# Second attention: when TensorE takes up the values of a quad, one quad behind each place or two behind every second

## The chip, the cores and the metric

The kernel runs on one core of a Trainium2 chip. The metric is the device time of one execution in microseconds (us); for the kernel before it is the median of three runs. One further execution was profiled.

## The reference, cut to what matters

Two layers, each with an attention and a feed-forward part. The change lies in the second layer's attention: two batches of 1,024 tokens, 32 heads of 16, one key and one value head shared by all, causal.

```python
def _L1_attn_ref(x, wq, wk, wv, wo):
    B, T, C = x.shape                      # 2, 1024, 512
    q = (x @ wq).reshape(B, T, 32, 16)
    k = x @ wk                             # one key head of 16
    v = x @ wv
    scores = jnp.einsum('bqhd,bkd->bhqk', q, k) * scale
    scores = jnp.where(causal[None, None], scores, -jnp.inf)
    probs = jax.nn.softmax(scores.astype(jnp.float32), axis=-1)
    out = jnp.einsum('bhqk,bkd->bqhd', probs, v).reshape(B, T, C)
    return out @ wo
```

## The kernel before, in words

The program has four stages, one behind the other: an opening with the first attention (to about 1160 us), a middle part, the second attention (`attention1`, from 1463 us, with its exponentials from 1500 to 2021 us), and a closing part.

`attention1` works in 16 **steps** (`STEPS1`), each four heads of one batch. A step has 12 **quads** (`QUADS`), one for each pair of half of the queries (`qc`, 512 columns) and key tile of 128 rows (`kt`) that the causal mask leaves: quads 0 to 3 have `qc` 0, quads 4 to 11 have `qc` 1. On the diagonal the width falls: quads 0 to 3 are 512, 384, 256 and 128 query columns wide, quads 4 to 8 are 512 wide, and quads 9, 10 and 11 are 384, 256 and 128.

Four kinds of work meet on a quad:

- **Maxima** (`maximum`, L1769 and L1774): scores with the queries as rows, written to one of two double banks `as_mxp`, from which VectorE takes a row maximum (L1707 where the whole width is below the diagonal, L1709 elsewhere). They are made 32 tiles ahead, for the next step, two in each place.
- **Scores** (`score`, L1752, with L1754 and L1755 for the mask): keys as rows, one of three banks `as_scp`. A quad has four of them, one for each head (two in quads 2, 3, 10 and 11, which take two heads in one bank). ScalarE takes the exponential of each into a ring `as_prob` of 24 (L1659).
- **Values** (`values`, L1793): per quad, four matmuls of 32 columns of the array side by side, one for each head, from `as_prob` into `as_op`. The type is float32, and the trace shows eight matmuls for a quad.
- **The copy out** (`copy_out`, L1666): `as_op` is a single bank. When the values of quad 3 and of quad 11 are in, ScalarE copies it to `as_u_sb`. The values of quads 0 and 4 (`kt == 0`) overwrite the bank, so they wait for that copy: `pe.wait_ge(s["u_copied"], 2 * t + qc)`.

The order on each engine is written out by hand. TensorE goes through 192 **places** (`QSETS`, index `g`; `n` is `g` modulo 12). A place is: a maximum, two scores, a maximum, two scores (maxima of the coming step, scores of quad `n`), and behind them values of earlier quads, by the lines that the change touches. ScalarE has its own list:

```python
for n in range(QUADS):
    if n == TURN_AT and t + 1 < STEPS1:
        maxima_out(t + 1)
    exps(t, n)
    if n == 2 and t >= 1:
        copy_out(t - 1, 1)
    if n == 6:
        copy_out(t, 0)
```

So the copy for quads 4 to 11 of the step before stands behind the exponentials of quad 2, and the copy for quads 0 to 3 behind the exponentials of quad 6. Score `x` waits until the exponential of score `x - 3` is done, maximum `u` until VectorE is done with maximum `u - 2`.

Of the kernel before, what the change touches and what calls it, by code (L numbers as in the profile page):

```python
# [600 lines left out]
QUADS = UNITS // G  # L601
# [972 lines left out]
def attention1(nc, k, q_dram, sums, recips, stale, queries_in, next_loads):  # L1574

    with ExitStack() as ctx:
# [22 lines left out]
        with nc.Block() as block:  # L1599
# [130 lines left out]
            def _(pe):  # L1730
                def score(t, n, j):
                    qc, kt = QK[n]
                    x = t * SCORES1 + FIRST1[n] + j
                    c0 = max(kt - 4 * qc, 0) * P
                    w = HALF - c0
                    jj, both = j % 2, UNITS1_OF[n] == 2
                    rows, group = slice(RG * jj, RG * jj + MAXROW + 1), slice(RG * jj, RG * (jj + 1))
                    if both:
                        out = scp[x % BANKS1][:, 0:PAIRS * w].rearrange("p (i c) -> p i c", i=PAIRS)
                        queries = q[t % SLOTS1][rows, :, HALF * qc + c0:HALF * (qc + 1)]  # L1740
                        block = out[:, :, 0:P]
                        after = lambda part: k.tri[group, 2 + part, :].unsqueeze(1).to_broadcast([RG, PAIRS, P])
                    else:
                        s0 = min(c0, HALF - 2 * P)
                        out = scp[x % BANKS1][:, s0:HALF]
                        queries = q[t % SLOTS1][rows, j // 2, HALF * qc + s0:HALF * (qc + 1)]
                        block = scp[x % BANKS1][:, c0:c0 + P]
                        after = lambda part: k.tri[group, 2 + part, :]
                    diagonal = kt >= 4 * qc
                    if x >= BANKS1:  # L1750
                        pe.wait_ge(s["exp_done"], x + 1 - BANKS1)
                    mm = nc.tensor.matmul(out, k.keys[rows, t // NG, kt * P:(kt + 1) * P], queries, start=True, stop=not diagonal)  # L1752
                    if diagonal:
                        nc.tensor.matmul(block, k.tri[group, 0, :], after(0), start=False, stop=False)  # L1754
                        mm = nc.tensor.matmul(block, k.tri[group, 1, :], after(1), start=False, stop=True)  # L1755
                    mm.then_inc(s["sc_ready"], 1)

                def maximum(u):
                    t, (i, qt, part) = u // MSTEP, MPAIRS[u % MSTEP]
                    full = qt >= 4 and part == 0  # L1760
                    k0 = HALF if qt >= 4 and part == 1 else 0
                    w = HALF if full else (qt % 4 + 1) * P
                    if u % MSTEP == 0:
                        pe.wait_ge(q_in[t % SLOTS1], MOVES * (t // SLOTS1 + 1))
                    freed(pe, ("max", u))
                    tile = mxp[banks["max", u][0]]
                    for jj in range(2):
                        rows = slice(RG * jj, RG * jj + MAXROW)
                        mm = nc.tensor.matmul(tile[:, jj, 0:max(w, 2 * P)], q[t % SLOTS1][rows, i, qt * P:(qt + 1) * P],  # L1769
                                              k.keys[rows, t // NG, k0:k0 + max(w, 2 * P)], start=True, stop=full)  # L1770
                    for half in () if full else range(2):
                        for jj in range(2):
                            group = slice(RG * jj, RG * (jj + 1))
                            mm = nc.tensor.matmul(tile[:, jj, w - P:w], k.tri[group, half, :], k.tri[group, 4 + half, :],  # L1774
                                                  start=False, stop=(half == 1))
                    mm.then_inc(s["mx_ready"], 1)

                def turn_maxima(t):
                    pe.wait_ge(s["mx_joined"], t + 1)
                    freed(pe, ("turn", t))  # L1780
                    nc.tensor.transpose(mxp[banks["turn", t][0]][0:G * TILES, 0, 0:P], mxd[:, t % 2].rearrange("p j i q -> p (j i q)"),
                                        k.ident[:]).then_inc(s["mt_ready"], 1)

                def values(t, n):
                    qc, kt = QK[n]
                    c0 = max(kt - 4 * qc, 0) * P
                    x = t * SCORES1 + FIRST1[n]
                    pe.wait_ge(s["exp_done"], x + UNITS1_OF[n])
                    if kt == 0 and 2 * t + qc > 0:
                        pe.wait_ge(s["u_copied"], 2 * t + qc)  # L1790
                    for j in range(G):
                        p0 = c0 if UNITS1_OF[n] == G else j // 2 * (HALF - c0)
                        mm = nc.tensor.matmul(op[2 * HD * j:2 * HD * (j + 1), c0:HALF], k.vn[:, t // NG, kt, :],  # L1793
                                              prob[:, (x + j % UNITS1_OF[n]) % RING1, p0:p0 + HALF - c0],
                                              start=(kt == 0), stop=(kt == 4 * qc + 3))
                    mm.then_inc(s["pv_done"], 1)
# [3 lines left out]
                for g in range(QSETS):  # L1800
                    t, n = divmod(g, QUADS)
                    if n == TURN_AT and t + 1 < STEPS1:
                        turn_maxima(t + 1)
                    if n == 0:
                        pe.wait_ge(m_in[t % SLOTS1], 32 * (t // SLOTS1 + 1))
                    mine = range(LEAD + MQUAD * g, min(LEAD + MQUAD * (g + 1), MSTEP * STEPS1))
                    for i in range(MQUAD):
                        for u in mine[i:i + 1]:
                            maximum(u)
                        for j in range(2 * i, min(2 * i + 2, UNITS1_OF[n])):  # L1810
                            score(t, n, j)
                    if g % 2 and g >= 3:
                        values(*divmod(g - 3, QUADS))
                        values(*divmod(g - 2, QUADS))
                for g in (QSETS - 2, QSETS - 1):
                    values(*divmod(g, QUADS))
# [303 lines left out]
```

## Time and profile before

| | |
|---|---|
| median of three runs | 2172.82 us (2171.63 to 2172.96) |
| the profiled execution, its own time | 2168.36 us |
| its span, first to last instruction | 2166.6 us |
| TensorE busy | 1990.0 us, 92% of the span |
| VectorE, ScalarE, GpSimd busy | 1161.2, 885.1 and 480.5 us |
| mean granted TensorE clock | 0.944 of full speed |

The span has 34,181 instructions. The profile calls TensorE's matmuls PE and its weight loads PEld, VectorE DVE, ScalarE ACT, GpSimd POOL. "Busy" of PE is the union of matmuls whose ends are modelled, so its idle time is better read as the distance between the starts of its instructions. In a timeline row the first number is the start, the second the length of the merged group, xN the number of instructions in it, and a bracket at the end tells the idle time ahead of it and what ended that.

### The profile page before, as it was taken

What the parts mean: (1) busy time and instruction counts of PE and PEld (TensorE: products, weight loads), DVE (VectorE), ACT (ScalarE), POOL (GpSimd) and SP (SyncE); (2) the same over time, 40 slices, a digit from 0 to 9 for tenths busy, and PEclk for the clock granted to TensorE, in tenths of its full rate; (3) what the DMA queues carried; (4) which work ended last, traced back from release to release, by engine and by line L of the source; (5) the groups of instructions that cost most, each with busy time, mean ns of one, the idle gap of its engine ahead of it and who ended that gap; (6) DMA issues with size and microseconds to landing.
All of it is one profiled execution on the core that took longest, in us unless ns stands there. A gap on an engine that the chain in (4) does not pass through costs nothing. (4 is left out here: it accounts for less than half of the span.)

```text
span 2166.6 us, 34181 instructions
## 1 busy us (share of the span) xinstructions
PE 1990.0 (92%) x12648; PEld 1151.5 (53%) x12648; DVE 1161.2 (54%) x2541; ACT 885.1 (41%) x1877; POOL 480.5 (22%) x376
## 2 busy tenths in 40 slices
PE   5859999999999999999967999988999999999698
PEld 4535666666666666666634454544444444444244
DVE  3536655555555555555402445437667667663166
ACT  3413344444444444444431222222666666666222
POOL 0014245555444444455330000000000000000000
PEclk8869999999999999999988999995999999998799
DMA  9742233222233323332135211153223212211201
GB/s 311 263 143 59 60 79 80 66 59 56 68 80 80 79 70 80 79 80 62 39 119 179 73 63 48 60 132 93 42 33 52 47 33 52 47 18 27 89 29 49
DMA packets 113592, 172.19 MB, mean 79 GB/s; under 512 B 26186, under 2 KB 46826, under 8 KB 113298
## 3 DMA queue, kind: packets, MB, share of 16 engines
q1 hardware_dynamic: 112402, 169.75, 29.7%
q8 instruction: 100, 1.64, 0.3%
q14 instruction: 66, 0.54, 0.1%
q10 hardware_dynamic: 1024, 0.26, 0.1%
HBM read 84.32 MB, written 29.38 MB: 52 GB/s over the span
## 5 line engine op out<-in xcount | busy, mean ns | idle before, releaser
L886 ACT ACTIVATE at_prob<-at_scp 128x512 f32<-128x512 f32 (+1 forms) x608 | 349.8, 576 | 515.5 <-PE at_scp L989 514.3
L1659 ACT ACTIVATE as_prob<-as_scp 128x512 f32<-128x512 f32 (+2 forms) x640 | 309.0, 563 | 200.2 <-PE as_scp L1755 148.9
L921 DVE CUSTOM_DVE_ANT_0 at_junk<-at_mxp,causal 128x128 f32<-128x128 f32 (+3 forms) x512 | 243.6, 488 | 189.9 <-PE at_mxp L1000 185.2
L1709 DVE TENSOR_REDUCE as_mxd<-as_mxp 128x2 f32<-128x256 f32 (+3 forms) x256 | 203.5, 821 | 98.3 <-PE as_mxp L1774 96.0
L916 DVE TENSOR_REDUCE at_mxf<-at_mxp 128x1 f32<-128x512 f32 x256 | 176.1, 688 | 142.7 <-PE at_mxp L1000 138.9
L1694 POOL TENSOR_TENSOR l_att_t<-l_att_t,as_spread 64x1024 f32<-64x1024 f32 x16 | 37.9, 2367 | 861.5 <-DMA as_spread<-l_recips 861.5
L1707 DVE TENSOR_REDUCE as_mxf<-as_mxp 128x2 f32<-128x1024 f32 x128 | 151.0, 1221 | 60.3 <-PE as_mxp L1769 60.1
L816 POOL TENSOR_TENSOR at_pre<-at_prob 128x512 f32<-128x512 f32 x64 | 80.2, 1282 | 409.8 <-ACT at_prob L886 409.8
L816 POOL TENSOR_TENSOR at_pre<-at_pre,at_prob 128x512 f32<-128x512 f32 x128 | 160.6, 1285 | 3.6 <-ACT at_prob L886 1.2
L1793 PE MATMUL as_op<-as_prob,l_vn 128*32 128x512 f32 (+3 forms) x1536 | 160.4, 540 | 0.0
L985 PE MATMUL at_scp<-hd_early_q,l_khi 97*128 97x512 f32 (+1 forms) x304 | 138.1, 454 | 10.9 <-DMA hd_late_q<-at_slo 8.2
L1022 PE MATMUL at_op<-at_prob,l_cn 128*32 128x512 f32 (+3 forms) x1536 | 143.7, 491 | 4.0 <-ACT at_u_sb L857 4.0
L985 PE MATMUL at_scp<-at_qhi,l_khi 97*128 97x512 f32 (+1 forms) x304 | 138.7, 456 | 0.8 <-ACT at_prob L886 0.5
L1000 PE MATMUL at_mxp<-l_khi,hd_early_q 96*128 96x512 f32 (+2 forms) x384 | 125.6, 381 | 10.2 <-DMA hd_early_q<-at_shi 8.9
L1000 PE MATMUL at_mxp<-l_khi,at_qhi 96*128 96x512 f32 (+2 forms) x384 | 122.5, 367 | 0.5 <-DVE at_mxf L916 0.2
L988 PE MATMUL at_scp<-hd_late_q,l_khi 96*128 96x512 f32 (+1 forms) x304 | 118.4, 389 | 0.0
L989 PE MATMUL at_scp<-hd_early_q,l_klo 96*128 96x512 f32 (+1 forms) x304 | 118.0, 388 | 0.0
L988 PE MATMUL at_scp<-at_qlo,l_khi 96*128 96x512 f32 (+1 forms) x304 | 116.8, 384 | 0.0
L989 PE MATMUL at_scp<-at_qhi,l_klo 96*128 96x512 f32 (+1 forms) x304 | 116.3, 383 | 0.0
L1769 PE MATMUL as_mxp<-l_keys,hd_early_q 48*128 48x512 f32 (+2 forms) x384 | 97.7, 488 | 19.2 <-DVE as_mxf L1707 7.3
L1752 PE MATMUL as_scp<-as_q,l_keys 49*128 49x512 f32 (+2 forms) x320 | 108.1, 463 | 7.8 <-ACT as_prob L1659 6.4
L1752 PE MATMUL as_scp<-hd_early_q,l_keys 49*128 49x512 f32 (+2 forms) x320 | 103.7, 446 | 5.7 <-ACT as_prob L1659 4.3
(232 smaller groups left out, 3352.8 us busy)
## 6 DMA issues: line engine op xcount, KB each, us to landing
hd_late_q<-at_slo SPq DMA_DIRECT2D x96, 128.0 KB, 2.4
at_qhi<-at_shi SPq DMA_DIRECT2D x96, 128.0 KB, 2.4
at_qlo<-at_slo SPq DMA_DIRECT2D x96, 128.0 KB, 2.4
hd_early_q<-at_shi SPq DMA_DIRECT2D x84, 128.0 KB, 2.5
at_spread<-l_recips SPq DMA_DIRECT2D x64, 128.0 KB, 2.8
l_o<-at_u_sb SPq DMA_DIRECT2D x16, 512.0 KB, 3.3
hd_early<-in_wmod SPq DMA_DIRECT2D x7, 1024.0 KB, 7.8
hd_late<-l_o SPq DMA_DIRECT2D x12, 512.0 KB, 4.4
```

The source lines that it names most:

```text
L816: nc.gpsimd.tensor_tensor(pre[:, j, :], other, prob[:, (x + j) % RING0, :], ALU.add).then_inc(s["pre_done"], 1)
L886: nc.scalar.activation(prob[:, x % RING0, c0:HALF], scp[x % BANKS0][:, c0:HALF], ACT.Exp).then_inc(s["exp_done"], 1)
L916: nc.vector.reduce_max(mxf[:, j, qt - 4:qt - 3], tile[:], AX_X).then_inc(s["mx_done"], 1)
L921: nc.vector.tensor_tensor_reduce(out=junk[:, u % 2, 0:w], in0=tile[:, 0:w], in1=k.causal[:, HALF - w:HALF], scale=1.0, scalar=LOWEST, op0= ...
L985: nc.tensor.matmul(out, k.khi[0:KR + 1, b, ks], q_cols(qhi[t % 2][0:KR + 1]), start=True, stop=False)
L988: nc.tensor.matmul(out, k.khi[0:KR, b, ks], q_cols(qlo[t % 2][0:KR]), start=False, stop=False)
L989: nc.tensor.matmul(out, k.klo[0:KR, b, ks], q_cols(qhi[t % 2][0:KR]), start=False, stop=True).then_inc(s["sc_ready"], 1)
L1000: nc.tensor.matmul(bank("max", t, u)[:, 0:w], qhi[t % 2][0:KR, qt // 4, j, qt % 4 * P:(qt % 4 + 1) * P], k.khi[0:KR, t // NG, k0:k0 + w], ...
L1659: nc.scalar.activation(prob[:, x % RING1, cols], scp[x % BANKS1][:, cols], ACT.Exp).then_inc(s["exp_done"], 1)
L1709: nc.vector.reduce_max(mxd[:, t % 2, :, i, qt:qt + 1], tile[:, :, 0:(qt % 4 + 1) * P], AX_X).then_inc(s["mx_done"], 1)
L1752: mm = nc.tensor.matmul(out, k.keys[rows, t // NG, kt * P:(kt + 1) * P], queries, start=True, stop=not diagonal)
L1793: mm = nc.tensor.matmul(op[2 * HD * j:2 * HD * (j + 1), c0:HALF], k.vn[:, t // NG, kt, :], prob[:, (x + j % UNITS1_OF[n]) % RING1, p0:p0 + ...
```

## The change

Before, a place with odd `g` ended with the values of the two quads `g - 3` and `g - 2`, and one with even `g` had no values. After, every place from `g` = 2 on ends with the values of quad `g - 2`. Nothing else is changed; ScalarE, VectorE, GpSimd and the DMA queues issue what they did, in the order they did.

```diff
                         for j in range(2 * i, min(2 * i + 2, UNITS1_OF[n])):
                             score(t, n, j)
-                    if g % 2 and g >= 3:
-                        values(*divmod(g - 3, QUADS))
+                    if g >= 2:
                         values(*divmod(g - 2, QUADS))
                 for g in (QSETS - 2, QSETS - 1):
                     values(*divmod(g, QUADS))
```

TensorE's order in places 6 and 7 of a step, before. L1769 and L1774 are maxima, L1752 scores, L1793 the values, here of quads 4 and 5 together:

```order
L1769 MATMUL as_mxp<-l_keys,hd_early_q 128x512 x2
L1752 MATMUL as_scp<-hd_early_q,l_keys 128x512 x2
L1769 MATMUL as_mxp<-l_keys,hd_early_q 128x512 x2
L1752 MATMUL as_scp<-hd_early_q,l_keys 128x512 x2
L1769 MATMUL as_mxp<-l_keys,hd_early_q 128x512 x2
L1774 MATMUL as_mxp<-l_tri 128x128 x4
L1752 MATMUL as_scp<-hd_early_q,l_keys 128x512 x2
L1769 MATMUL as_mxp<-l_keys,hd_early_q 128x512 x2
L1774 MATMUL as_mxp<-l_tri 128x128 x4
L1752 MATMUL as_scp<-hd_early_q,l_keys 128x512 x2
L1793 MATMUL as_op<-as_prob,l_vn 32x512 x8
```

And the same two places as they are now:

```order
L1769 MATMUL as_mxp<-l_keys,hd_early_q 128x512 x2
L1752 MATMUL as_scp<-hd_early_q,l_keys 128x512 x2
L1769 MATMUL as_mxp<-l_keys,hd_early_q 128x512 x2
L1752 MATMUL as_scp<-hd_early_q,l_keys 128x512 x2
L1793 MATMUL as_op<-as_prob,l_vn 32x512 x4
L1769 MATMUL as_mxp<-l_keys,hd_early_q 128x512 x2
L1774 MATMUL as_mxp<-l_tri 128x128 x4
L1752 MATMUL as_scp<-hd_early_q,l_keys 128x512 x2
L1769 MATMUL as_mxp<-l_keys,hd_early_q 128x512 x2
L1774 MATMUL as_mxp<-l_tri 128x128 x4
L1752 MATMUL as_scp<-hd_early_q,l_keys 128x512 x2
L1793 MATMUL as_op<-as_prob,l_vn 32x512 x4
```

The values of quad 4 have moved from the end of place 7 to the end of place 6, right behind the scores of quad 6; those of quad 5 stay at the end of place 7.

ScalarE's order over one step, which is the same before and now: the exponentials of quad 2, a copy out, those of quad 3, those of quads 4, 5 and 6, the other copy out, those of quads 7 and 8, and the row of maxima:

```order
L1659 ACTIVATE as_prob<-as_scp 128x512 x2
L1666 ACTIVATE as_u_sb<-as_op 128x512
L1659 ACTIVATE as_prob<-as_scp 128x256 x2
L1659 ACTIVATE as_prob<-as_scp 128x512 x12
L1666 ACTIVATE as_u_sb<-as_op 128x512
L1659 ACTIVATE as_prob<-as_scp 128x512 x8
L1672 ACTIVATE as_mrow<-as_mxp 32x128
```

Here nothing moved: the copy that the values of quad 4 wait for stands behind the last exponential of quad 6, and the one that the values of quad 0 wait for behind the last of quad 2.

## Rows read from the trace of the kernel before

**Rows 1.** Costliest groups: the exponentials; busy us, mean ns, idle before, released by

```profile
L1659 ACT ACTIVATE as_prob<-as_scp 128x512 f32<-128x512 f32 (+2 forms) x640 | 309.0, 563 | 200.2 <-PE as_scp L1755 148.9
```

**Rows 2.** Two steps, by stretches: busy PE, PEld, DVE, ACT, POOL; clock, DMA

```profile
1566.00:1598.00 32.00, 30.19 (x306) 15.71 (x304) 22.60 (x27) 20.27 (x44) 4.55 (x2) 1.00 0.31 49
1598.00:1631.00 33.00, 31.20 (x299) 15.42 (x297) 21.98 (x27) 20.14 (x43) 2.16 (x2) 0.95 0.26 43
```

**Rows 3.** Timeline of PE, places 4 and 5 of one step, values at both ends

```profile
1605.12 1.71 PE L1793 MATMUL as_op<-as_prob,l_vn 128*32 128x512 f32 x16
1606.76 0.50 PE L1769 MATMUL as_mxp<-l_keys,hd_early_q 48*128 48x512 f32 x2
1607.10 0.40 PE L1752 MATMUL as_scp<-as_q,l_keys 49*128 49x512 f32 x2
...
1608.24 0.49 PE L1752 MATMUL as_scp<-as_q,l_keys 49*128 49x512 f32 x1 [0.27 <-ACT as_prob L1659]
1608.59 0.44 PE L1769 MATMUL as_mxp<-l_keys,hd_early_q 48*128 48x384 f32 x2
...
1610.63 0.86 PE L1793 MATMUL as_op<-as_prob,l_vn 128*32 128x256 f32 x16
1611.42 0.50 PE L1769 MATMUL as_mxp<-l_keys,hd_early_q 48*128 48x512 f32 x2
1611.75 0.39 PE L1752 MATMUL as_scp<-as_q,l_keys 49*128 49x512 f32 x2
```

**Rows 4.** Timeline of ACT, places 2 to 6 of the same step

```profile
1603.76 0.60 ACT L1666 ACTIVATE as_u_sb<-as_op 128x512 f32<-128x512 f32 x1
1607.59 4.16 ACT L1659 ACTIVATE as_prob<-as_scp 128x512 f32<-128x512 f32 x8 [2.38 <-PE as_scp L1752]
1612.24 2.07 ACT L1659 ACTIVATE as_prob<-as_scp 128x512 f32<-128x512 f32 x4 [0.49 <-PE as_scp L1752]
1614.17 0.63 ACT L1666 ACTIVATE as_u_sb<-as_op 128x512 f32<-128x512 f32 x1
```

**Rows 5.** Timeline of PE, places 2 and 3 of the same step

```profile
1602.06 0.40 PE L1752 MATMUL as_scp<-as_q,l_keys 49*128 49x512 f32 x2
...
1602.45 0.48 PE L1769 MATMUL as_mxp<-l_keys,hd_early_q 48*128 48x512 f32 x2
1603.54 0.38 PE L1769 MATMUL as_mxp<-l_keys,hd_early_q 48*128 48x256 f32 x2 [0.61 <-DVE as_mxf L1707]
1603.77 0.29 PE L1774 MATMUL as_mxp<-l_tri 64*128 64x128 bf16 x4
1603.87 0.36 PE L1752 MATMUL as_scp<-as_q,l_keys 49*128 49x256 f32 x2
...
1604.90 0.29 PE L1774 MATMUL as_mxp<-l_tri 64*128 64x128 bf16 x4
```

**Rows 6.** Timeline of PE: starts of places 2, 4, 6, 8, 10, 0, 2

```profile
1634.98 0.50 PE L1769 MATMUL as_mxp<-l_keys,hd_early_q 48*128 48x512 f32 x2
...
1640.02 0.50 PE L1769 MATMUL as_mxp<-l_keys,hd_early_q 48*128 48x512 f32 x2
...
1644.68 0.50 PE L1769 MATMUL as_mxp<-l_keys,hd_early_q 48*128 48x512 f32 x2
...
1650.88 0.39 PE L1769 MATMUL as_mxp<-l_keys,as_q 48*128 48x256 f32 x2
...
1657.18 0.44 PE L1769 MATMUL as_mxp<-l_keys,as_q 48*128 48x384 f32 x2
...
1661.87 0.50 PE L1769 MATMUL as_mxp<-l_keys,as_q 48*128 48x512 f32 x2
...
1666.61 0.50 PE L1769 MATMUL as_mxp<-l_keys,as_q 48*128 48x512 f32 x2
```

**Rows 7.** Timeline of PE: values of quads 4 and 5 at lower clock, next place

```profile
1615.93 3.39 PE L1793 MATMUL as_op<-as_prob,l_vn 128*32 128x512 f32 x16
1619.25 0.38 PE L1769 MATMUL as_mxp<-l_keys,hd_early_q 48*128 48x256 f32 x2
```

## The prediction

> **What bounds the kernel now.** The time is that of one stage, so I read, in this order, the stretches by engine, the groups, and the timelines of TensorE and ScalarE over single places. A step of the second attention takes 31.6 us, or 33.3 where the clock drops in it. In 32 us TensorE has matmuls in flight for 30.2, VectorE works 22.6 and ScalarE 20.3 [rows 2]. So TensorE paces the stage, but not at its peak: it waits for the two others, and they wait for it in bursts: ScalarE's exponentials waited 200 us in all, most of it for masked scores [rows 1].
>
> The timelines show why. Take places 4 and 5 [rows 3]. After values the first score starts 0.34 us into the place, at 1607.10. Its exponential starts at 1607.59, where ScalarE had been idle for 2.38 us [rows 4]. The fourth score needs the first one's bank and starts at 1608.24, 1.14 us behind the first. From there ScalarE is the pace: eight exponentials take 4.16 us without a gap. Then TensorE does the values, and ScalarE runs dry.
>
> Six pairs of places make a step. By their starts [rows 6] the pairs that begin with places 2, 4, 6, 8, 10 and 0 take 5.04, 4.66, 6.20, 6.30, 4.69 and 4.74 us, 31.63 in all.
>
> **The change, part by part.** No instruction is added or taken away; half of the values move one place forward. Four things follow.
>
> *1. More blocks of values.* There were 95 blocks (the last one joined with the tail), now there are 190. What does a block cost beside its columns? The one of 512 and 384 columns runs from 1605.12 to 1606.76, 1.64 us, the one of 256 and 128 from 1610.63 to 1611.42, 0.79 [rows 3]. The 512 more columns make 0.85 us, so 384 make 0.64, and 0.15 is left for each block. The way in: from L1774 to a score takes 0.10 us (1603.77 to 1603.87), from L1774 to values 0.22 (1604.90 to 1605.12) [rows 3, 5], so 0.12 more. Together 0.27 us a block, 25.7 us for 95 blocks if nothing hides it.
>
> A rule of the Trainium skill bears on this price ("TensorEngine Tiling (Array Packing)", Key Properties): a change of tiling mode drains the array, which is the case between a score and values, since these use other shapes of the array. By the rule all 190 new changes cost; by the rows those into values cost nothing where the values wait anyway, which is 31 times 0.12, or 4 us, less than the rule taken alone.
>
> *2. A new wait.* This is the largest term. The values of quad 4 may start only when ScalarE has copied `as_op` out, and ScalarE does that behind the exponentials of quad 6. Before, they came at the end of place 7, when the copy was long done. Now they stand at the end of place 6. Place 6 began at 1611.42, its first score at 1611.75 [rows 3]; its exponentials began at 1612.24, and the copy ran from 1614.17 to 1614.80 [rows 4]. That is 3.05 us behind the first score, and with 0.05 us for the release (the difference of the 1.14 above to 0.49 and a 0.60 us exponential) the values could start at 3.10. Without the copy they could start at 1.14 + 0.35 (score to next instruction, 1608.24 to 1608.59 [rows 3]) + 0.12 = 1.61. TensorE, which is in order, stands 1.5 us. Behind it wait the next maxima, scores and everything else, and ScalarE and VectorE run dry behind the copy.
>
> The same in place 2: quad 0's values wait for the copy behind the exponentials of quad 2. First score 1602.06, copy 1603.76 to 1604.36 [rows 4, 5], so values at 2.35 us. Without it they could follow the second maximum (1602.45 [rows 5]) by some 0.45 us, at 0.84. Again 1.5 us.
>
> There are 16 such waits in place 6 and 15 in place 2 (none in the first step): 31 times 1.5 is 47 us.
>
> *3. Less starving.* This is the gain. A place that follows a short block finds ScalarE and VectorE less empty. I don't take a price from one row but lay the new places out from the rows, from first maximum to first maximum. A full place with values of 512 columns is 0.34 + 1.14 + 0.47 + 0.85 + 0.15 = 2.95 us. Places 6 and 2 are 0.34 + 3.10 + 0.85 + 0.15 = 4.44 and 0.34 + 2.35 + 0.85 + 0.15 = 3.69. Place 7 has longer masked maxima, 3.05. Places 4 and 5, with 256 and 128 columns of values (0.43, 0.21), come to 2.5 and 2.3. So the pair of places 4 and 5 is 4.8 (4.66 before), the pair 6 and 7 is 7.5 (6.20), the pair 2 and 3 is 3.69 + 1.9 = 5.6 (5.04). The pairs with masked scores come out, laid out in the same way, at 6.4 for 8 and 9 (6.30), 4.4 for 10 and 11 (4.69) and 5.0 for 0 and 1 (4.74). The sum is 33.7 us a step against 31.63, so +2.1. Of that the two waits are +3.0, the blocks +1.6, and the rest, -2.5, is less starving; VectorE binds hardly anywhere now, where before TensorE waited 0.61 us for it [rows 5]. Fifteen steps' worth: +31 us. The old order laid out in this way gives 31.4 where 31.63 was measured, so I trust the step to some 0.4 us, which is 6 us in all.
>
> *4. The clock.* Where the pair of places 6 and 7 falls badly, the clock goes to 1.2 GHz: its values took 3.39 us, and the pair 7.83 (1611.42 to 1619.25) [rows 3, 7] against 6.20, 1.63 us more. The step has a granted clock of 0.95 against 1.00 [rows 2]. Seven steps of 16 are so. It fell after 4.5 us without any values, matmuls on 48 or 49 rows alone. The new order's longest stretch without values is shorter, 3.6 us in place 6, but TensorE stands for a good part of it. I take half of the seven as gone: -6 us, with bounds of -11 (none left) and +15 (one in each step).
>
> DMA, VectorE and GpSimd issue what they did; the copies come at the same places, so nothing downstream is later by itself. The closing part is untouched.
>
> **Sum.** +31 - 6 = +25. Against the profiled execution's own 2168.36 us that makes 2193; the median of the runs is 4.5 us above that execution, so 2197 for the median.
>
> **The rivals.**
>
> *The even flow wins (faster).* If the copy cost no wait, the step would be 33.7 - 3.0 = 30.7 us, 0.9 under before, and with the clock drops gone 15 times 0.9 plus 11 is -25 us: 2148. For it speaks that ScalarE stood 2.38 us after a pair of values [rows 4]. Against it: the copy's place in ScalarE's list is written out, and both copies' ends are rows. It decides if the wait in places 2 and 6 is below 0.45 us each rather than 1.5. 4 in 100.
>
> *The wait is there, but half of it is caught up (slightly slower).* Behind the wait the maxima find free banks at once, and later places may run shorter than laid out, by 0.8 us for each wait: +31 - 25 - 6, about 0, so 2173; with the drops left as they were, 2179. 8 in 100, of which 3 fall within 0.2% and 1 below.
>
> *The clock turns worse (slower still).* TensorE now stands for 1.5 us twice a step beside its shorter waits. If the clock drops in every step, that is +31 + 15 = +46: 2219. The Trainium skill ("TensorE: Matmul & The Clock Gate", A second HAM failure mode: psum-queue depth-cycling) says that short idle times between groups of matmuls can make the clock swing. Before, waits of 0.3 to 0.6 us in nearly every place [rows 3, 5] left most steps at full clock [rows 2], which speaks for less. 14 in 100.
>
> **How the numbers follow.** The forecast (two new waits a step, the rest roughly as laid out, +12 to +38) has 74 in 100, the rivals 26. The range takes in the step's 6 us either way and the clock's bounds, and reaches to the third rival: 2184 to 2215. About 0.2%, 4.3 us, is what a measurement of this kernel tells from no change. Faster by more than that: the first rival and 1 of the second, 0.05. Within: 3 of the second and 1 of the forecast's own lower end, 0.04. Slower: 0.91.
>
> **What the changed profile would show.** 190 blocks of values. Two waits a step of TensorE for ScalarE at L1793 that are released by L1666, about 1.5 us each, 31 in all. Steps of about 33.7 us at full clock. ScalarE's idle time before a place's first exponential near 1 us and nowhere 2.4, but for the place after the copy. Places 6 and 2 of 4.4 and 3.7 us, full places of 2.95. Wrong would be the sum if L1793 waits for L1666 for under half a microsecond, if TensorE waits for VectorE in many places, or if the steps vary by 1.6 us with the clock in more than four cases.

## The result, and the profile after

The changed kernel takes 2285.04 us (median of four runs, 2283.4 to 2290.1) against 2172.23, a ratio of 1.053 (95% interval 1.052 to 1.054): slower by 113 us. Forecast were 2197 us and a range that ended at 2215. The sign was right, the size was wrong by 88 us. The ratios here and below, but not the medians, leave out executions that took over 1.5% more than the fastest of their kernel: one of the kernel before (2320 us), one of e1 (3337), one of e4 (4890) and two of e10 (2239 and 2262).

Where it went: the waits list of the profile after has the new wait, at the size that was forecast, and longer waits of VectorE and ScalarE for TensorE. (Who waits, for whom: us in total, times, longest. In the kernel before the first two rows were 88.8 and 148.9 us.)

```profile
DVE as_mxd L1709 <- PE as_mxp L1774: 208.3, 154, 3.7
ACT as_prob L1659 <- PE as_scp L1755: 203.9, 141, 3.7
PE as_op L1793 <- ACT as_u_sb L1666: 48.5, 31, 1.8
```

The values waited 31 times for the copy, 48.5 us; the prediction had 31 times and 47 us. The groups answer to [rows 1] with ScalarE's idle time up from 200 to 293 us, and show the values themselves at 210.7 us where they had 160.4:

```profile
L1659 ACT ACTIVATE as_prob<-as_scp 128x512 f32<-128x512 f32 (+2 forms) x640 | 311.6, 556 | 293.4 <-PE as_scp L1755 208.4
L1793 PE MATMUL as_op<-as_prob,l_vn 128*32 128x512 f32 (+3 forms) x1536 | 210.7, 627 | 48.5 <-ACT as_u_sb L1666 48.5
```

The same matmuls take longer because many of them run at a lower clock. By stretches (columns as in [rows 2]), the changed kernel, over 500 us of the stage, then from the wait in place 2 to the end of place 11 of one step, and then 16 us of that, from the start of place 8:

```profile
1510.00:2010.00 500.00, 450.27 (x3725) 208.04 (x3723) 284.82 (x327) 260.51 (x542) 25.98 (x11) 0.82 0.20 34
...
1624.40:1659.70 35.30, 32.06 (x232) 14.18 (x232) 17.85 (x21) 16.26 (x34) 2.35 (x1) 0.71 0.09 18
...
1642.00:1658.00 16.00, 16.00 (x105) 7.31 (x103) 4.58 (x8) 5.27 (x11) 2.35 (x1) 0.50 0.07 18
```

and the kernel before over the same 500 us:

```profile
1510.00:2010.00 500.00, 472.09 (x4431) 235.83 (x4423) 320.46 (x374) 311.97 (x662) 35.53 (x15) 0.95 0.22 38
```

The granted clock of these 500 us is 0.82 against 0.95, and 0.50, the lower of its two levels (1.2 GHz), from place 8 into place 11 of this step. The values of quad 0, in place 2 of this step and of the next, stand 42.2 us apart, where 33.7 were forecast for a step:

```profile
1625.36 1.06 PE L1793 MATMUL as_op<-as_prob,l_vn 128*32 128x512 f32 x8 [1.58 <-ACT as_u_sb L1666]
...
1667.58 1.06 PE L1793 MATMUL as_op<-as_prob,l_vn 128*32 128x512 f32 x8 [1.58 <-ACT as_u_sb L1666]
```

This is one of the longer steps. The twelve between 1551.59 and 2023.78 took 35.4 to 44.6 us. TensorE's timeline shows where the clock falls, places 6 to 9 of one step of the changed kernel:

```profile
1633.10 0.50 PE L1769 MATMUL as_mxp<-l_keys,hd_early_q 48*128 48x512 f32 x2
1633.43 0.40 PE L1752 MATMUL as_scp<-as_q,l_keys 49*128 49x512 f32 x2
...
1634.58 0.49 PE L1752 MATMUL as_scp<-as_q,l_keys 49*128 49x512 f32 x1 [0.28 <-ACT as_prob L1659]
1636.63 1.07 PE L1793 MATMUL as_op<-as_prob,l_vn 128*32 128x512 f32 x8 [1.56 <-ACT as_u_sb L1666]
1637.63 0.50 PE L1769 MATMUL as_mxp<-l_keys,hd_early_q 48*128 48x512 f32 x2
...
1640.29 1.94 PE L1793 MATMUL as_op<-as_prob,l_vn 128*32 128x512 f32 x8
1642.16 0.58 PE L1769 MATMUL as_mxp<-l_keys,hd_early_q 48*128 48x256 f32 x2
...
1645.45 1.93 PE L1793 MATMUL as_op<-as_prob,l_vn 128*32 128x512 f32 x8
1647.32 0.40 PE L1781 MATMUL as_mxp<-ident,as_mxd 128*32 128x128 f32 x1
```

Place 6 is as laid out: first score at 1633.43, values at 1636.63, 3.20 us behind it (3.10 forecast), 1.56 us of it standing. Then the values of quad 5 take 1.94 us where those of quad 4 took 1.07, and place 8 takes 5.16 us (1642.16 to 1647.32). ScalarE in the same places answers to [rows 4]:

```profile
1633.93 2.06 ACT L1659 ACTIVATE as_prob<-as_scp 128x512 f32<-128x512 f32 x4 [0.20 <-PE as_scp L1752]
1635.86 0.63 ACT L1666 ACTIVATE as_u_sb<-as_op 128x512 f32<-128x512 f32 x1
1638.92 2.29 ACT L1659 ACTIVATE as_prob<-as_scp 128x512 f32<-128x512 f32 x4 [2.43 <-PE as_scp L1752]
```

Four exponentials, the copy to 1636.49, and then 2.43 us with nothing to do, since the scores stand behind the values.

### The profile page after: what moved, and what is told of

It is laid out like the page before. It is cut to its first block and busy times, and to the rows that moved or that the text cites. A ratio compares the mean times of both kernels' runs of the same rounds, so it can differ in the third digit from the quotient of the medians.

```text
span 2281.6 us, 34181 instructions
## 1 busy us (share of the span) xinstructions
PE 2071.3 (91%) x12648; PEld 1165.0 (51%) x12648; DVE 1167.2 (51%) x2541; ACT 892.6 (39%) x1877; POOL 480.2 (21%) x376
## 5 line engine op out<-in xcount | busy, mean ns | idle before, releaser
L1793 PE MATMUL as_op<-as_prob,l_vn 128*32 128x512 f32 (+3 forms) x1536 | 210.7, 627 | 48.5 <-ACT as_u_sb L1666 48.5
L816 POOL TENSOR_TENSOR at_pre<-at_pre,at_prob 128x512 f32<-128x512 f32 x128 | 160.4, 1282 | 3.6 <-ACT at_prob L886 1.2
L1752 PE MATMUL as_scp<-as_q,l_keys 49*128 49x512 f32 (+2 forms) x320 | 114.9, 541 | 7.1 <-ACT as_prob L1659 6.8
L1769 PE MATMUL as_mxp<-l_keys,hd_early_q 48*128 48x512 f32 (+2 forms) x384 | 104.8, 532 | 13.0 <-PEq L1215 4.7
L1752 PE MATMUL as_scp<-hd_early_q,l_keys 49*128 49x512 f32 (+2 forms) x320 | 108.3, 497 | 6.0 <-ACT as_prob L1659 5.3
```

Source lines behind the costliest of these rows:

```text
L816: nc.gpsimd.tensor_tensor(pre[:, j, :], other, prob[:, (x + j) % RING0, :], ALU.add).then_inc(s["pre_done"], 1)
```

## The experiments

Two theories were tried against each other. **W**: the waits for the copy are the cause, by their own 48 us and because TensorE stands in them and the clock falls. **B**: more and shorter blocks of values bring the clock down, waits or not. Ratios are to the kernel before, run together with each.

**e1 and e5: the copy earlier.** In `exps`, the copy behind the first exponential of quads 2 and 6:

```diff
                         nc.scalar.activation(prob[:, x % RING1, cols], ...).then_inc(s["exp_done"], 1)
+                        if i == 0 and n == 2 and t >= 1:
+                            copy_out(t - 1, 1)
+                        if i == 0 and n == 6:
+                            copy_out(t, 0)
```

(and the two calls behind `exps` taken out.) Expected:

> The changed order, one quad of values behind each place, but ScalarE copies the bank of values out behind the first exponential of quads 2 and 6 instead of the last. Theory W (the two waits for the copy bring the clock down, and cost 48 us by themselves): no wait of L1793 for L1666 above 0.3 us, steps of about 31 us, lower clock in at most half of the steps, 2150 to 2175 us. Theory B (more and shorter blocks of values bring the clock down, waits or not): the 48 us of waits go, the clock of the stage stays near 0.85, 2220 to 2245 us.

Measured: 2177.95 us, ratio 1.004 (1.002 to 1.006). The execution that was profiled is the one of 3337 us, so for its profile the kernel was run once more:

> The kernel of e1 once more, for its profile. Steps near 31 us at full clock and near 32 us on average, no wait of L1793 for L1666 above 0.3 us, clock of the stage 0.93 or more; 2170 to 2185 us.

One execution, 2166.33 us, clock of the same 500 us 0.97:

```profile
PE as_op L1793 <- ACT as_u_sb L1670: 16.5, 15, 1.3
```

The wait in place 6 is gone. The 15 in place 2 are not, they are 1.1 us instead of 1.6: there only two exponentials stand ahead of the copy, and one of them is still ahead. So "no wait above 0.3 us" was wrong, and a step at full clock is 32.1 us, not 31; the single execution of e5 lies 4 us under its range. The time of e1 lies 3 us above W's bound and 42 us below B's. All 190 blocks are in this kernel, so blocks alone don't bring the clock down.

**e2: quads 0 and 4 held back.** Single blocks but for places 3 and 7:

```diff
-                    if g >= 2:
+                    if g >= 2 and n not in (2, 6):
+                        if n in (3, 7):
+                            values(*divmod(g - 3, QUADS))
                         values(*divmod(g - 2, QUADS))
```

> The changed order, but the values of quads 0 and 4 stay one place back, with those of quads 1 and 5, as in the kernel before; all others single. No wait for the copy, 158 blocks of values instead of 190. Theory W: 2155 to 2180 us. Theory B: two thirds of the clock's share stay, 2205 to 2230 us.

Measured: 2178.68 us, 1.004 (1.003 to 1.005), clock 0.944 over the whole kernel as before. W again, and without any change to ScalarE's list. It also says what the even flow is worth by itself with the values at the end of a place: nothing, rather 0.4% less than the pairs.

**e3: the waits alone.** The kernel before, with the values of quads 0 and 4 one place forward:

```diff
+                    if g >= 2 and n in (2, 6):
+                        values(*divmod(g - 2, QUADS))
                     if g % 2 and g >= 3:
-                        values(*divmod(g - 3, QUADS))
+                        if n not in (3, 7):
+                            values(*divmod(g - 3, QUADS))
                         values(*divmod(g - 2, QUADS))
```

> The kernel before, with only the values of quads 0 and 4 one place forward: both waits for the copy, 127 blocks of values. Theory W: waits and clock as in the changed kernel, 2250 to 2290 us. Theory B: the waits' own 48 us and little of the clock, 2210 to 2230 us.

Measured: 2247.49 us, 1.034 (1.032 to 1.036), clock of the same 500 us 0.83 in its slowest execution (2261 us), which is the one profiled. Above B's bound by 17 us, and 3 us under W's. So two moved quads of twelve bring 76 of the 113 us, far more than the 47.7 us that its waits have; the clock follows the wait also where the other values come in pairs, if a little less.

**e4: the copy earlier in the kernel before.** The edit of e1 on the kernel before.

> The kernel before with the copy out behind the first exponential of quads 2 and 6. Nothing waits for that copy in the order of before, so both theories expect no change: 2167 to 2178 us. A change here would mean that the copy's place acts by itself (a later exponential), and e1 would have to be read with it.

Measured: 2170.62 us, 1.000 (0.999 to 1.001). The copy's place does nothing by itself; what e1 wins it wins by the wait.

**e6 and e7: one wait each.** The edit of e1 for quad 6 alone, and for quad 2 alone.

> The changed order with the copy early in quad 6 alone, so that the wait in place 2 stays (15 waits) and the one in place 6 goes. If each wait brings its share of the clock: half of the 107 us between the changed kernel and e1, 2220 to 2240 us. If the wait in place 6 is the one behind the clock (it follows the two short blocks of quads 2 and 3): 24 us of waits alone stay, 2195 to 2215 us. If the one in place 2 is: 2245 to 2265 us.

> The mirror of e6: the wait in place 6 stays (16 waits), the one in place 2 goes. Shares alike: 2220 to 2240 us. Place 6 behind the clock: 2245 to 2265 us. Place 2 behind it: 2195 to 2215 us.

Measured: e6 (the wait in place 2 stays) 2192.14 us, 1.009 (1.008 to 1.011). e7 (the wait in place 6 stays) 2267.10 us, 1.046 (1.041 to 1.051). In e7 the wait in place 2 is not gone, it is 1.1 us as in e5. The waits of e6, and of e7 below them:

```profile
PE as_op L1793 <- ACT as_u_sb L1668: 23.9, 15, 1.8
```

```profile
PE as_op L1793 <- ACT as_u_sb L1668: 41.2, 31, 1.6
```

The same 500 us of e6, and of e7 below it:

```profile
1510.00:2010.00 500.00, 461.99 (x4318) 217.30 (x4320) 329.00 (x377) 301.70 (x633) 30.74 (x13) 0.95 0.21 36
```

```profile
1510.00:2010.00 500.00, 456.22 (x3834) 211.72 (x3834) 293.55 (x335) 266.90 (x555) 28.40 (x12) 0.83 0.20 34
```

Both waits are about equally long (e6 has 15 of 1.6 us), but with the one in place 2 the clock is 0.95, with the one in place 6 it is 0.83. e7 and e1 differ by the wait in place 6 alone: 16 waits of 1.55 us, 25 us, and 89 us in time. So the wait in place 6 is the one behind the clock. Both results lie just past the bounds that were expected for this (3 us under, 2 us over).

**e9 and e10: the wait kept, TensorE kept busy in it.** Does the clock fall because TensorE stands, or from something that comes with the wait? In place 6, ahead of the waiting values:

```diff
+                def fill(u, count):
+                    t, (i, qt, part) = u // MSTEP, MPAIRS[u % MSTEP]
+                    freed(pe, ("max", u))
+                    tile = mxp[banks["max", u][0]]
+                    for _ in range(count):
+                        for jj in range(2):
+                            rows = slice(RG * jj, RG * jj + MAXROW)
+                            nc.tensor.matmul(tile[:, jj, :], q[t % SLOTS1][rows, i, qt * P:(qt + 1) * P],
+                                             k.keys[rows, t // NG, 0:HALF], start=True, stop=True)
...
+                    if n == 6 and LEAD + MQUAD * (g + 1) < MSTEP * STEPS1:
+                        fill(LEAD + MQUAD * (g + 1), 6)
                     if g >= 2:
```

> The changed kernel, and in place 6, behind the scores and ahead of the waiting values, six pairs of matmuls of 512 columns that write the bank which the next maximum then overwrites: the same wait for the copy, but TensorE is busy in it (6 times 0.235 = 1.4 us of the 1.6 us). They compute nothing that is used. If the clock falls because TensorE stands still there: the clock's share of place 6 (e7's 95 us less 24 us of waits, some 70 us) goes, 2205 to 2230 us. If it falls for another reason (the pattern of short blocks ahead, or the wait's effect on the other engines): 2275 to 2295 us.

> The same with three pairs, 0.7 us of the wait. If idle time counts in proportion: halfway, 2240 to 2260 us. If it is a threshold: either near e9 or near the changed kernel.

Measured, six pairs: 2200.52 us, 1.013 (1.011 to 1.015), 5 us under the bound of the first reading. Work was added, and 85 us went. Its timeline, places 6 to 8, and the values of quad 0 of this step and the next:

```profile
1690.51 1.66 PE L1785 MATMUL as_mxp<-l_keys,as_q 48*128 48x512 f32 x12
1692.21 1.07 PE L1803 MATMUL as_op<-as_prob,l_vn 128*32 128x512 f32 x8
1693.21 0.50 PE L1769 MATMUL as_mxp<-l_keys,as_q 48*128 48x512 f32 x2
...
1696.29 0.39 PE L1769 MATMUL as_mxp<-l_keys,as_q 48*128 48x256 f32 x2
...
1699.51 0.28 PE L1791 MATMUL as_mxp<-ident,as_mxd 128*32 128x128 f32 x1
...
1715.01 1.07 PE L1803 MATMUL as_op<-as_prob,l_vn 128*32 128x512 f32 x8 [1.57 <-ACT as_u_sb L1666]
...
1749.10 1.06 PE L1803 MATMUL as_op<-as_prob,l_vn 128*32 128x512 f32 x8 [1.58 <-ACT as_u_sb L1666]
```

The twelve matmuls fill the wait and end as the values start. Place 8 takes 3.22 us (1696.29 to 1699.51) where it took 5.16, and a step 34.09 (1715.01 to 1749.10). The clock of the 500 us is 0.99:

```profile
1510.00:2010.00 500.00, 462.60 (x4471) 223.87 (x4467) 324.44 (x373) 300.58 (x629) 30.75 (x13) 0.99 0.21 36
```

The copy comes as late as in the changed kernel, and the values start 3.18 us behind the first score (1689.03 to 1692.21) as they did there (3.20), so the clock's share there comes from TensorE standing, not from what the late copy does to the other engines. e9 by itself can't tell TensorE's standing from too little work in the stretch, since it adds work. But e1 and e6 take this wait away, add nothing, and also keep the clock up (0.97 and 0.95).

With three pairs (e10) the four runs took 2191, 2218, 2239 and 2262 us at granted clocks of 0.951, 0.936, 0.927 and 0.913. The median of the four is 2228.45, 1.026 of the kernel before; the two faster ones alone give 1.016 (1.009 to 1.022), which leaves open whether it is slower by 2%. The fastest is the one profiled. TensorE still stands for 0.74 us in its place 6, and its clock is 1.00:

```profile
1688.88 0.96 PE L1785 MATMUL as_mxp<-l_keys,as_q 48*128 48x512 f32 x6
1690.59 1.07 PE L1803 MATMUL as_op<-as_prob,l_vn 128*32 128x512 f32 x8 [0.74 <-ACT as_u_sb L1666]
```

```profile
1510.00:2010.00 500.00, 452.73 (x4413) 215.34 (x4409) 325.16 (x374) 302.38 (x634) 30.73 (x13) 1.00 0.21 37
```

So half of the filling let the clock hold in one run, and the others ran at a lower mean clock. Neither of the two expectations had that. The slower runs have no profile, so where their clock fell is not shown.

**e8 and e11: values in the middle of a place.** Can the even flow be had better? The values three quads back, behind the first two scores, with the copy early (e8) or late as before (e11):

```diff
                         for j in range(2 * i, min(2 * i + 2, UNITS1_OF[n])):
                             score(t, n, j)
-                    if g >= 2:
-                        values(*divmod(g - 2, QUADS))
-                for g in (QSETS - 2, QSETS - 1):
+                        if i == 0 and g >= 3:
+                            values(*divmod(g - 3, QUADS))
+                for g in (QSETS - 3, QSETS - 2, QSETS - 1):
```

> The values of one quad in each place, but in its middle, behind the first two scores and three quads back, with the copy early. The last two scores of a place wait 0.67 us for the first exponential there, and the values' 0.85 us would fill that. If TensorE's wait for ScalarE's first exponential is what bounds a full place: full places of about 2.3 to 2.5 us instead of 2.95, steps of 27 to 29 us, 2110 to 2145 us. If VectorE becomes the bound (2.44 us of maxima in half of the places) or the clock falls more often: 2145 to 2180 us.

> e8 with the copies out behind the last exponentials of quads 2 and 6, as in the kernel before. The values of quads 0 and 4 now stand in the middle of places 3 and 7, so the wait for the copy should be short, 0.2 to 0.6 us. If what helps in e8 is the values' place in the middle: 2150 to 2165 us. If it is the early copy: 2165 to 2200 us, and by the reading of e9 only more if TensorE's standing there brings the clock down.

Measured: e8 2153.97 us, 0.992 (0.990 to 0.994), faster than both kernels, if by less than 1% of the kernel before. e11 2170.29, 1.000 (0.998 to 1.002). The stage in e8, and in e11 below it:

```profile
1510.00:2010.00 500.00, 485.74 (x4541) 220.54 (x4541) 326.46 (x377) 323.03 (x677) 35.55 (x15) 0.97 0.22 38
```

```profile
1510.00:2010.00 500.00, 480.98 (x4453) 218.61 (x4445) 324.66 (x375) 317.60 (x664) 35.55 (x15) 0.95 0.22 38
```

The waits for the copy are 9.3 us in 17 times in e11, and one of 0.3 us in e8:

```profile
PE as_op L1793 <- ACT as_u_sb L1666: 9.3, 17, 0.6
```

The hope of 2110 to 2145 us for e8 failed: its steps are 31.1 us, not 27 to 29. It lies in the second range, 2145 to 2180, but not because the clock fell more often (0.97 against 0.95 before). Between the second and the third exponential of a place ScalarE now stands, by 1.0 to 1.2 us in places 7 to 9, since the values are between the second and the third score. The idle time was moved more than filled. e11 lies in the range for the early copy being what helps; but e1 has the early copy too, with the values at the end of a place, and took 2178. So neither change alone wins, and the two together do. Against e8, e11 has short waits and a lower clock (0.95), which go with its 16 us more; how they share them is not shown.

## Why the prediction was wrong, point by point

- **The count and the price of blocks** (part 1): right. 190 blocks. At full clock the places came as laid out: 8 and 9 together 6.43 us in e9 (6.4 forecast), 10 and 11 together 4.42 (4.4), and places 4 and 5 in the changed kernel 2.48 and 2.39 (2.5 and 2.3).
- **The new wait** (part 2): right in place, number and size. 48.5 us in 31 waits (47 forecast). It was found in ScalarE's list and priced by the row of a copy that in the kernel before nobody waited for. e3 (the wait without the other blocks) and e4 (the early copy where nobody waits) show it from both sides.
- **Less starving** (part 3): right for a step, within the 0.4 us that was given to it. At full clock a step takes 34.07 us in e9 and e10, 33.7 was worked out. Over the stage the parts ahead of the clock are +39 us (16 steps by 2.44, 34.07 less 31.63) where the sum had +31 (15 by 2.1).
- **The clock** (part 4): this is the step that failed. The prediction took half of the seven drops as gone, -6 us, with +15 (a drop in each step) as the worst. In the same terms the runs show some +74: the 113 us less the 39 above. e9 bears this out. It has the order and the late copies of the changed kernel and nearly no drop, so it should be 39 less the 11 of the seven drops of before, 28 us above 2172, and 2200.5 was measured. The changed kernel is 85 us above that, 5.3 us for each step. It is also what its trace has: the twelve steps from 1551.59 to 2023.78 took 39.3 us in the mean, against 34.07, and none of them under 35.4. So there was a drop in each of these steps, and the prediction's own sign of being wrong (steps that vary by 1.6 us with the clock in more than four cases) came.

Two errors are in that term. The sign: the prediction saw that TensorE would stand in a long stretch without values, called the stretch shorter than the one of before, and halved the drops. The stretch is shorter (3.53 us, 1633.10 to 1636.63, where its own terms give 3.44 and the text 3.6; before it was 4.5), and yet the clock falls behind it; e9 shows that the standing in it was what mattered. The size: it priced a drop at 1.63 us, that of one pair of values at the lower clock, and at most one in a step. But in the changed kernel the clock can stay down over several places, for 20 us in the step shown: place 8 alone is 5.16 instead of 3.22 us, places 9 and 10 took 5.16 and 4.27 instead of 3.21 and 2.31 in e9. The third rival named the mechanism and had 14 in 100, but with the same price for a drop, so even it ended at 2219.

The rule of the Trainium skill that stood behind this rival ("TensorE: Matmul & The Clock Gate", A second HAM failure mode: psum-queue depth-cycling) says that TensorE's short idle times between groups make the clock swing and cost throughput. The trace and e9 agree with it here. The numbers are 1.56 us of standing in each step with a clock of 0.82, and 0.99 with the standing filled. The prediction held against it that waits of 0.3 to 0.6 us had left most steps at full clock; that is no evidence for 1.6 us.

The drain rule of the Trainium skill ("TensorEngine Tiling (Array Packing)", Key Properties) says that a change of tiling mode drains the array. It has no figure. The trace agrees that the way into values costs more than the way into a score, 0.21 us (1627.24 to 1627.45) against 0.09 (1626.58 to 1626.67):

```profile
1626.58 0.29 PE L1774 MATMUL as_mxp<-l_tri 64*128 64x128 bf16 x4
1626.67 0.36 PE L1752 MATMUL as_scp<-as_q,l_keys 49*128 49x256 f32 x2
...
1627.24 0.29 PE L1774 MATMUL as_mxp<-l_tri 64*128 64x128 bf16 x4
1627.45 0.85 PE L1793 MATMUL as_op<-as_prob,l_vn 128*32 128x384 f32 x8
```

What all 95 more blocks cost is not isolated by any run. e1 has them and the rest of the waits, and is 0.4% slower than the kernel before; so these costs together are a little more than the even flow wins.

What stays open: why the wait in place 6 brings the clock down for long and the equal one in place 2 hardly (e6). It can't be the short blocks of values ahead of it by themselves, which the expectation of e6 offered: both places follow a block of 256 and one of 128 columns (at 1630.14 and 1632.74 ahead of place 6, at 1619.65 and 1622.22 ahead of place 2). What differs is the rest, masked scores in places 0 and 1 and unmasked ones in places 4 and 5; whether that is the reason was not tried. In e9's profile the clock held in all but two of the thirteen steps from 1540.41 to 1987.60 (36.7 and 35.7 us, the others 34.1); with half the filling it held in e10's profile and less in its other runs.

## What to carry to other kernels

Moving a consumer forward moves it relative to every engine's written list, not only to its input: look for the release that stands behind something else there, and price it by the row of the releasing instruction even if nobody waits for it yet. Where a change makes TensorE stand in each round, as the 1.56 us in place 6 did here, don't price the wait alone; give the clock its own case, with everything behind the wait at the lower level, for it can cost more than the wait (here some 74 us against 48). Releasing a single bank behind the first of four exponentials instead of the last, and putting the values where TensorE would wait, turned a loss of 5.3% into a gain of 0.8%.

## What the runs showed of the hardware that was not expected

- Twelve matmuls whose results are thrown away, put in a wait of 1.6 us in 15 of the 16 steps, made the changed kernel 85 us faster (e9). The granted clock went from 0.82 to 0.99 over 500 us of the stage.
- With half as many the same program spread over 71 us in four runs (2191 to 2262), its time following its granted clock (0.951 to 0.913), where the kernel before, run together with it, spread over 6. Four runs are few for that.
- Two waits of TensorE that are equally long, 1.55 and 1.58 us, 11 us apart in the same loop, act on the granted clock very differently: 0.83 with the one (e7), 0.95 with the other (e6).
- At the lower clock the whole place stretches, not the values alone: the values took 1.94 us instead of 1.07, and place 8 took 5.16 instead of 3.22.
